# The node stage of a graph layer on one core: per-block sums and 1/std kept in a PSUM bank, copied to the SBUF tables every four blocks

## The reference, cut to what matters

```python
h = jnp.maximum(_layernorm(x, axis=-1), 0.0)          # mean, variance, eps 1e-5
edge_in_f = concat([h[src], h[dst], edge_features])
msgs_f = relu(edge_in_f @ W1_f + b1_f) @ W2_f + b2_f  # and msgs_r with src and dst exchanged
agg = segment_sum(msgs_f, dst) + segment_sum(msgs_r, src)
node_in = concat([agg, h])
out = x + h + relu(node_in @ Wn1 + bn1) @ Wn2 + bn2
```

## Time and profile before

| | |
|---|---|
| time, median of 3 runs | 1625.49 us |
| the profiled execution's own time | 1627.22 us |
| its span, first to last instruction | 1625.5 us |
| TensorE busy | 1318.5 us (81%) |
| VectorE busy | 972.4 us (60%) |
| ScalarE busy | 944.0 us (58%) |
| GpSimd busy | 1120.1 us (69%) |
| mean granted TensorE clock | 0.835 of full |

### The profile page before, as it was taken

The page is one execution under the profiler, slowest core; times in us unless marked ns, Lnnn a source line. Parts: engine busy times, 40 slices in busy tenths (PEclk is TensorE's granted clock), DMA queues, the critical chain, the costliest instruction groups (busy, mean ns, idle before and its releaser), DMA issues.

```text
span 1625.5 us, 29085 instructions
## 1 busy us (share of the span) xinstructions
PE 1318.5 (81%) x7070; PEld 997.1 (61%) x7070; DVE 972.4 (60%) x2902; ACT 944.0 (58%) x2256; POOL 1120.1 (69%) x1003
## 2 busy tenths in 40 slices
PE   6988998457787788887877887878888865899998
PEld 4777776345565666665656665656666654666665
DVE  7999998336666666666665666666666641222222
ACT  5888888244555455555545555455555533677776
POOL 7899878888888888888888888888888862000000
PEclk9999999567878777778787778787777777999999
DMA  7999998335555555555545555555555546999998
GB/s 222 310 312 315 315 312 280 101 59 108 103 109 108 107 104 103 102 103 103 102 93 99 101 103 102 98 100 102 103 103 102 102 76 205 333 369 348 346 349 292
DMA packets 238374, 280.71 MB, mean 173 GB/s; under 512 B 53170, under 2 KB 155200, under 8 KB 238348
## 3 DMA queue, kind: packets, MB, share of 16 engines
q1 hardware_dynamic: 168408, 241.57, 44.7%
q0 software_dynamic: 68992, 38.59, 20.3%
q10 hardware_dynamic: 948, 0.30, 0.1%
HBM read 162.62 MB, written 117.72 MB: 172 GB/s over the span
## 4 chain that ended last, share of the span: by engine, by line
POOL 28%; issue 19%; DMA 15%; PE 9%; DVE 5%; ACT 1%; POOLq 0%; SPq 0%; DVEq 0%; another core or an unknown queue 0%; ACTq 0%
POOL table L532 24%; DMA out_x<-ncentred 12%; POOL got_odd L514 5%; DMA table<-to_send,scatter_at 3%; PE bank L846 3%; DVE ncentred L1137 2%; PE bank L820 2%; PE bank L818 2%; PE bank L833 1%; DVE same L979 1%; PE bank L871 1%; DMA same<-table 1%; PE bank L804 1%; PE bank L882 0%; DVE sums L961 0%
## 5 line engine op out<-in xcount | busy, mean ns | idle before, releaser
L532 POOL DMA_INDIRECT table<-to_send,scatter_at x392 | 640.9, 1635 | 134.1 <-issue 118.3
L846 PEld LDWEIGHTS bank<-message,same 128*128 128x128 f32 x1960 | 300.1, 243 | 47.1 <-issue 43.6
L846 PE MATMUL bank<-message,same 128*128 128x128 f32 x1960 | 322.4, 335 | 3.3 <-DVE message L1010 3.3
L639 ACT ACTIVATE nh<-nx,all_sums,all_rstd 128x64 f32<-128x64 f32 x784 | 280.2, 434 | 0.0
L514 POOL DMA_INDIRECT got_even<-in_x,gather_first x196 | 211.8, 1081 | 40.9 <-issue 36.1
L775 PE MATMUL bank<-wn_h,nturned 128*128 128x256 f32 x784 | 196.6, 394 | 26.9 <-ACT nhidden L683 18.4
L514 POOL DMA_INDIRECT got_odd<-in_x,gather_at x180 | 179.9, 999 | 54.8 <-issue 54.2
L818 PE MATMUL bank<-turned,w_ends 128*128 128x256 f32 x392 | 175.5, 540 | 37.8 <-ACT turned_edge L609 37.1
L804 PE MATMUL bank<-ident,h_ends 128*128 128x128 f32 x196 | 51.4, 355 | 184.4 <-DVE h_ends L1019 181.4
L1004 DVE TENSOR_TENSOR scatter_at<-moved,ids 128x4 int32<-128x4 f32 x98 | 16.0, 163 | 296.6 <-DMA table<-to_send,scatter_at 296.6
L775 PEld LDWEIGHTS bank<-wn_h,nturned 128*128 128x128 f32 x784 | 143.1, 192 | 63.3 <-issue 33.0
(11 more groups left out here) (78 smaller groups left out, 1971.0 us busy)
## 6 DMA issues: line engine op xcount, KB each, us to landing
nx<-in_x SPq DMA_DIRECT2D x194, 256.0 KB
table<-nhidden SPq DMA_DIRECT2D x97, 512.0 KB
same<-table SPq DMA_DIRECT2D x97, 512.0 KB, 5.3
others<-numbers SPq DMA_DIRECT2D x196, 128.0 KB
out_x<-ncentred SPq DMA_DIRECT2D x97, 256.0 KB, 4.4
nx<-out_x SPq DMA_DIRECT2D x55, 256.0 KB, 4.6
out_x<-nh SPq DMA_DIRECT2D x31, 256.0 KB
table<-to_send,scatter_at POOLq DMA_INDIRECT x392
```

Of the source, the lines that this page charges most:

```text
L532: pool.indirect_dma_start(table, bass.IndirectOffsetOnAxis(ap=scatter_at[s][:, k:k + 1], axis=0), to_send[s][:, k, :], None, compute_op=AL ...
L639: last = act.activation(nh[s][:, g, :], nx[place][:, g, :], ACT.Relu, bias=all_sums[:, at, g:g + 1].rearrange("p a g -> p (a g)"), scale=a ...
L846: last = pe.matmul(bank[6 + s][:, k * M:(k + 1) * M], same[s][:, o, k * P:(k + 1) * P], message[s][:, o, :], start=(o == k), stop=(o == KB ...
```

## The change: what it does

A part of PSUM bank 7 becomes two small rings, `some_sums` and `some_rstd`, each of four places (one for each block of a turn of the loop) of 8 numbers. `sum_begin` writes the sums into its place of the first, `invert_begin` the reciprocals into its place of the second, and `centre_begin` and `normal_begin` read them there. A new helper, `keep`, copies the four places to their rows of `all_sums` or `all_rstd` in SBUF with one VectorE instruction: for the sums in the first step of each turn, behind `centre_begin`; for 1/std in the second step of each turn, behind `normal_begin`. Two new semaphores say that a ring has been copied; `sum_begin` and `invert_begin` wait for them at place 0. The turned weights move from bank 7 to bank 6, for which TensorE waits until the edge numbers have been copied out of it.

```diff
--- before.py
+++ after.py
@@ -187,6 +187,8 @@
 
         ntab = [same[p // 2][:, :, :].rearrange("p a b -> p (a b)")[:, p % 2 * G * M:(p % 2 + 1) * G * M]
                 for p in range(NRING)]
+        some_sums = bank[7][:, 0:NRING * G].rearrange("p (w g) -> p w g", g=G)
+        some_rstd = bank[7][:, NRING * G:2 * NRING * G].rearrange("p (w g) -> p w g", g=G)
         all_sums = sb("all_sums", [P, NW, G])
         all_rstd = sb("all_rstd", [P, NW, G])
         ncentred = two("ncentred", [G, D])
@@ -266,6 +268,8 @@
         b_turned = sems("b_turned_ready")
         b_product = sems("b_product_done")
         b_rows = sems("b_rows_ready")
+        b_sums_kept = sem("b_sums_kept")
+        b_rstd_kept = sem("b_rstd_kept")
         b_stored = sems("b_rows_stored")
 
 
@@ -740,8 +744,9 @@
 
             def turn_weights():
                 pe.wait_ge(s_params, 16 * N_PARAMS)
+                pe.wait_ge(s_setup_ev, 2)
                 for end in (SRC, DST):
-                    last = pe.transpose(bank[7][:, end * M:(end + 1) * M], w2[:, end, :], ident[:, :])
+                    last = pe.transpose(bank[6][:, end * M:(end + 1) * M], w2[:, end, :], ident[:, :])
                 last.then_inc(s_setup_pe, 1)
 
             def weight_products():
@@ -925,7 +930,7 @@
                 for end in (SRC, DST):
                     dve.tensor_copy(b2_wide[:, end, :], b2[:, end:end + 1].to_broadcast([P, P])).then_inc(s_b2wide, 1)
                 dve.wait_ge(s_setup_pe, 2)
-                dve.tensor_copy(w2t[:, :, :].rearrange("p a m -> p (a m)"), bank[7][:, 0:2 * M]).then_inc(s_setup_ev, 1)
+                dve.tensor_copy(w2t[:, :, :].rearrange("p a m -> p (a m)"), bank[6][:, 0:2 * M]).then_inc(s_setup_ev, 1)
 
             def copy_weight_products():
                 dve.wait_ge(s_setup_pe, 3)
@@ -1048,19 +1053,17 @@
                 dve.tensor_tensor(to, nx[place][:, :, :], nh[s][:, :, :], ALU.add).then_inc(e_xh[s], 1)
 
 
-            def of_window(a, i, s):
-                return a[:, bass.ds(2 * i + s, 1), :].rearrange("p a g -> p (a g)")
-
             def sum_begin(i, s, turn, place):
                 dve.wait_ge(b_x[place], 16 * (turn + 1))
-                dve.tensor_reduce(of_window(all_sums, i, s), nx[place][:, :, :], AX.X, ALU.add).then_inc(b_sums[s], 1)
+                if place == 0 and not first(turn):
+                    dve.wait_ge(b_sums_kept, turn)
+                dve.tensor_reduce(some_sums[:, place, :], nx[place][:, :, :], AX.X, ALU.add).then_inc(b_sums[s], 1)
 
             def centre_begin(i, s, turn, place):
                 dve.wait_ge(b_sums[s], i + 1)
                 if not first(i):
                     dve.wait_ge(b_h[s], i)
-                of_all = of_window(all_sums, i, s)
-                dve.scalar_tensor_tensor(out=ncentred[s][:, :, :], in0=of_all.to_broadcast([P, G, D]),
+                dve.scalar_tensor_tensor(out=ncentred[s][:, :, :], in0=some_sums[:, place, :].to_broadcast([P, G, D]),
                                          scalar=-1.0 / D, in1=nx[place][:, :, :], op0=ALU.mult, op1=ALU.add
                                          ).then_inc(b_centred[s], 1)
 
@@ -1068,26 +1071,37 @@
                 dve.wait_ge(b_squared[s], i + 1)
                 dve.tensor_reduce(nvar[s][:, :], nsquares[s][:, :, :], AX.X, ALU.add).then_inc(b_var[s], 1)
 
-            def invert_begin(i, s):
+            def invert_begin(i, s, turn, place):
                 dve.wait_ge(b_std[s], i + 1)
-                dve.reciprocal(of_window(all_rstd, i, s), nstd[s][:, :]).then_inc(b_rstd[s], 1)
+                if place == 0 and not first(turn):
+                    dve.wait_ge(b_rstd_kept, turn)
+                dve.reciprocal(some_rstd[:, place, :], nstd[s][:, :]).then_inc(b_rstd[s], 1)
 
             def normal_begin(i, s, turn, place):
                 dve.wait_ge(b_rstd[s], i + 1)
-                of_all = of_window(all_rstd, i, s)
                 if not first(turn):
                     dve.wait_ge(b_turn[s], i - 1)
                 dve.scalar_tensor_tensor(out=nh[place][:, :, :], in0=ncentred[s][:, :, :], scalar=0.0,
-                                         in1=of_all.to_broadcast([P, G, D]), op0=ALU.max, op1=ALU.mult
+                                         in1=some_rstd[:, place, :].to_broadcast([P, G, D]), op0=ALU.max, op1=ALU.mult
                                          ).then_inc(b_h[s], 1)
+
+            def keep(to, of, kept, w, k):
+
+                if 0 <= w.least(k) < NW:
+                    n = min(NRING, NW - w.least(k))
+                    dve.tensor_copy(to[:, bass.ds(w.number(k), n), :], of[:, 0:n, :]).then_inc(kept, 1)
 
             def begin(w):
 
                 w.do(sum_begin, 3, ring=NRING)
                 w.do(variance_begin, 2)
                 w.do(centre_begin, 3, ring=NRING)
-                w.do(invert_begin, 2)
+                if w.n % NRING == 0:
+                    keep(all_sums, some_sums, b_sums_kept, w, 0)
+                w.do(invert_begin, 2, ring=NRING)
                 w.do(normal_begin, 2, ring=NRING)
+                if w.n % NRING == 1:
+                    keep(all_rstd, some_rstd, b_rstd_kept, w, -1)
                 if w.least() == 3:
                     copy_turned_weights()
                 if w.least() == 92:
@@ -1102,7 +1116,7 @@
                     Step(NW, 0).do(variance_begin, k)
                     if k == 0:
                         edge_columns()
-                    Step(NW, 0).do(invert_begin, k)
+                    Step(NW, 0).do(invert_begin, k, ring=NRING)
                     Step(NW, 0).do(normal_begin, k, ring=NRING)
             dve.memset(zeros, 0.0).then_inc(s_zeros, 1)
             run(dve, NW, [(4, 92, 4)], 0, begin)
@@ -1112,8 +1126,9 @@
             dve.wait_ge(s_setup_ev, 6)
             dve.wait_ge(s_const, 5)
             dve.wait_ge(s_table0, 16)
+            dve.wait_ge(b_sums_kept, -(-NW // NRING))
+            dve.wait_ge(b_rstd_kept, -(-NW // NRING))
             for s in range(2):
-                dve.wait_ge(b_rstd[s], NW // 2)
                 dve.wait_ge(b_turn[s], NW // 2)
             dve.scalar_tensor_tensor(out=all_sums[:, :, :], in0=all_sums[:, :, :], scalar=-1.0 / D,
                                      in1=all_rstd[:, :, :], op0=ALU.mult, op1=ALU.mult).then_inc(e_means, 1)
```

## The result

The changed kernel took 1727.57 us, median of 4 runs (1726.27 to 1731.68); the kernel before, beside it, 1629.2 (1623.82 to 1636.09, 4 runs). The ratio is 1.0618, with a 95% interval of 1.0595 to 1.0641: 98 us slower, where 25 us faster was forecast. The profiled execution took 1727.37 us for a span of 1725.6.

The account below looks back on a forecast made before the run. GpSimd's stream of gathers and memsets was taken to set the edge stage's start; removing 25.2 us of stalls, with VectorE's added 7.5 us hidden, gave 1625.5 - 25.2 = 1600.3 us, said as 1600, range 1595 to 1613.

Parts of the forecast that it names:

- the sum: Whole kernel: edge and last stages start 25.2 us sooner and run as long, giving 1600.3 us against the median.
- 37.4 us of cover: End of node stage: first join's matmuls over at 302.0, GpSimd's last memset at 339.4, so the arithmetic has that to spare.
- The rival "slower": VectorE's waits for PSUM writes add more than 0.38 us per block, overrunning the cover; 1632 us at 0.45; chance 0.04.
- The bound and the mechanism: GpSimd's 208 gathers and memsets set the edge stage's start; VectorE instructions with two SBUF inputs hold gathers.
- The stalls: Node-stage gathers held by L1063 and L1080: 25.2 us, all removed, so the last memset ends at about 314.1.
- a bound of about 4: TensorE's clock, less idle before the edge stage, may speed the first batch; bounded by about 4 us.
- the second form: L1080 reading SBUF then PSUM: taken as fully relieved, 13.0 us; rival that only the first form is: 1613, chance 0.10.
- The split 12.2 and 13.0: Gather stalls in the node stage: about 12.2 us by L1063 and 13.0 us by L1080.
- dear PSUM operands: Rival: VectorE's PSUM reads or writes cost extra and it takes over the path; 1602 to 1620 us, chance 0.16.
- The delay of the first join: Node stage's end: copies (5.5 us) and PSUM reads (2 us) on VectorE make it 7.5 us later, at about 309.5.
- The cover left: Between first join at about 309.5 and the gathers' end at 314.1: 4.6 us.
- TensorE's wait for bank 6, the semaphores of the rings: TensorE's wait for edge numbers costs nothing, hidden by parameter loads; VectorE's ring waits are already over when reached.

Follow-up runs that it names:

- short pause: The changed kernel with the memset behind each gather half as long (128 instead of 256 numbers): 1595.16 us on chip 8, ratio 0.9772 to before.
- long pause: The changed kernel with the memset behind each gather twice as long (512 numbers): 1655.28 us on chip 15, against 1628.03 before.

## Why the prediction was wrong, and where it was right

**The step that failed** is in the sum: "The edge and last stages start from the same state, 25.2 us sooner". It took the pace of the node stage's arithmetic as given, 37.4 us of cover less VectorE's 7.5 us. In the first comparison the arithmetic took 5.35 us for a block instead of 2.67, the last product began 142 us later, and the cover was overrun: the copy L629 went at 441.24 instead of 314. The rival "slower" had the right threshold (0.38 us more for each block) and the wrong place: it looked for it on VectorE, and VectorE was idle for half the time. The place is TensorE's completions reaching ScalarE, up to 9 us late. I had costed VectorE's and GpSimd's meeting only; that TensorE's signals could be held while GpSimd works was in no row that I had shown, and I had no rival for it. The trace of before did hold a hint in its records of semaphores: 28 completions late by up to 0.45 us in the node stage, and 14 by up to 1.9 us in the edge stage.

**The bound and the mechanism** stand. At each chip where completions were on time, GpSimd's stream sets the start of the edge stage: with the double memset L629 waits 54.6 us for it, with the half one not at all.

**The stalls**: forecast 25.2 us of relief, last memset at about 314.1. Measured on chip 8: stalls from 26.3 to 1.8 us, last memset at 314.10, L629 at 314.52 instead of 338.75; on chip 6: L629 at 314.17, stalls 1.2 us. The gain is 27.1 us by the medians on chip 8 (1631.97 - 1604.89) and 24.3 in the single run on chip 6. Of the 28.0 us between the spans of the two traces on chip 8, 24.2 are the earlier start; the other 3.8 are won behind it, which the sum had only as a bound of about 4. The 17 short gathers that the prediction puts into the first 0.03 us of an L1080 began 0.01 us before it, so they are no exception to its pattern. That the second form is relieved was chosen from what two rows had in common; the run with 1/std alone in PSUM shows it (stalls 26.3 to 8.1 us). The Trainium skill, SBUF, section "Who interferes with whom", which the prediction weighed for this, says that a VectorE instruction with at most one SBUF input, outside its two-port modes, doesn't contend with GpSimd; these runs agree. The split 12.2 and 13.0 was too small for each alone: either one alone took off more than 17 us, most likely because a gather that is no longer held moves those behind it. Together they can't take more than all 26.3.

**VectorE**: the 50 copies have a pitch of 0.10 us (118.33 to 118.43), forecast 0.11. L1066 and L1084, which read PSUM, have pitches of 0.60 (117.73 to 118.33, 118.75 to 119.35), and so has L1060, which writes PSUM (119.35 to 119.95, where the next instruction starts); forecast 0.60 to 0.62. So dear PSUM operands are out. The Trainium skill's 62 extra cycles for a PSUM source (VectorE: DVE Perf Modes, "The TRN2 errata") are not seen here; the measurement decides. The delay of the first join is the term that was mis-sized even where the forecast came true. On chip 8 the join was over at 305.48 us in the kernel before and at 301.78 in the changed one, and the node stage's last product began at 284.6 and 283.9. So the copies delay nothing that shows, where 7.5 us and a join at 309.5 were forecast. On all of the chips without the loss the first join of the unaltered changed kernel and of its short pause lies between 301.8 and 304.6. The cover left was 12 us and not 4.6, and ScalarE's wait at L629 was 13 to 14 us and not 9. Where 5 us of copies went I didn't test. VectorE's idle gaps are a likely place: from 40 to 270 us on chip 8 it ran 428 instructions in 223.51 us before and 470 in 225.09 after, in both for some 86 blocks.

**TensorE's wait for bank 6, the semaphores of the rings**: no wait on them is among the large ones in any trace.

**Cause of the loss, what is shown.** It is the same program at the same inputs (1605 on chips 6 and 8, 1731 on chip 11). It comes with TensorE's completions being counted late while GpSimd gathers, and it ends within about a microsecond of the last memset. The copies are not needed for it. The chip of the first comparison isn't recorded; it is like chip 11, the only one known to have the loss, in its late completions and in its number of semaphore records, and the trace of before shows that it was so without the change. The size of the loss follows: of the products' 784 matmuls, eight for each block, 456 are done by 312 us (busy time by stretch of L780), so 41 blocks are left, 41 x 2.7 = 111 us at full rate. The last product thus comes at about 312 + 111 = 423, 142 us after the 281.1 of before; less the cover of 37.4 that is 105 us for the edge stage's start, and 101.8 were measured.

**Argued only**: that at such a place the even stream of gathers is to blame, and that the stalls, which gave it gaps, had kept the lateness small before. For it speaks that the completions arrive at two fixed points of a gather, and that in all three traces with the loss a pause of GpSimd of 2.9 to 3.3 us put them on time, after which they were late again within 6 to 12 us although the gathers were no denser. That looks like something that piles up while gathers are issued and drains when they stop; nothing here shows what. On chips 6 and 8 the gathers are as even without a single late completion, so the even stream alone isn't enough.

**Open**: whether TensorE's work itself ends late or only its signal; whether the PSUM operands matter beside the pace, since 1/std alone and the long pause never ran on a chip with the loss; whether the missing semaphore records and the late completions have one cause, and whether the recording of the profile has a part in the loss, as every time given here is of a run with its span and clock recorded; and what differs between the chips.

## What to carry to other kernels

The cover that hides an engine's work is worth what its pace is worth: 37.4 us looked ample, and a stage that went at half its pace used it up nearly four times over. A change that makes one engine work more densely is a reason to price the pace of the others again, though that the density caused the loss here is not shown. A gain of 1.6% that was measured on one chip is not yet a gain: the same kernel ran from 1.6% faster to 6% slower across chips. The sign to look for is a waiting copy with "remote" as its releaser, while the matmuls before it are long over. A second one can be read before anything is changed: the traces of the kernel before, at two places, held 20,368 and 32,415 semaphore records. Where the loss is absent, shortening the filler behind each gather is worth a further 10 us (ratio 0.9772), until the first join becomes the bound; this version, the fastest measured, was not tried where completions are late.

## What the runs showed of the hardware that I had not expected

- TensorE's semaphore updates can be late, mostly by 2 to 9 us and once by 10.1, while GpSimd issues indirect DMAs 1.45 us apart (0.96 us each), and those of ScalarE and VectorE at the same time are not (0.01 us). They come through about 0.3 or 1.0 us behind the start of a gather. It happened in the first comparison and on chip 11, and not on chips 4, 6, 8 and 15. At the place of the first comparison the kernel before had it too, by up to 0.45 us beside gathers and 1.9 us beside scatters.
- Where it happens, the trace holds some 20,000 semaphore records instead of 32,400, and in the trace of before the missing ones are all from the time in which GpSimd issues indirect DMAs.
- The granted clock followed: 0.75 of full from 40 to 270 us and 0.99 where completions were on time, so the wait goes with a second cost, matmuls at a mix of the two levels (1.2 and 2.4 GHz; eight in up to 3.78 us instead of 1.99).
- One SBUF input with one from PSUM, in either order, leaves a gather at 0.96 us, where two from SBUF hold it for up to 0.5 us more.
- VectorE takes 0.60 us for 512 float32 numbers in each partition with or without an operand in PSUM.
